# Early tiles of a routed two-layer network: row loads, pads, releases, and one expert's weight split on another engine

## The reference

```python
z = _layernorm(x, ln_g, ln_b)
logits = jnp.einsum('bth,he->bte', z, rW) + rb          # 8 experts
topv, topi = jax.lax.top_k(softmax(logits), 2)
w = mask / denom                                        # weights of the two chosen
hid = jax.nn.gelu(jnp.einsum('bth,ehf->btef', z, W1) + b1, approximate=False)
outs = jnp.einsum('btef,efh->bteh', hid, W2) + b2
mixed = jnp.sum(outs * w[..., None], axis=2)
return x + mixed
```

## Time and profile before

| | us |
|---|---|
| median of 3 runs | 565.91 (563.12 to 567.77) |
| the profiled execution | 563.68 |
| its span, first to last instruction | 561.6 |
| TensorE busy | 449.8 (80%) |
| DVE busy | 442.2 (79%) |
| ACT busy | 377.1 (67%) |
| POOL busy | 268.0 (48%) |
| mean granted TensorE clock | 0.930 |

### The profile page before, as it was taken

The page is one execution under the profiler, slowest core; times in us unless marked ns, Lnnn a source line. Parts: engine busy times, 40 slices in busy tenths (PEclk is TensorE's granted clock), DMA queues, the critical chain, the costliest instruction groups (busy, mean ns, idle before and its releaser), DMA issues.

```text
span 561.6 us, 11667 instructions
## 1 busy us (share of the span) xinstructions
PE 449.8 (80%) x2730; PEld 387.5 (69%) x2730; DVE 442.2 (79%) x1492; ACT 377.1 (67%) x928; POOL 268.0 (48%) x195
## 2 busy tenths in 40 slices
PE   0296899967999978588668999999999999999100
PEld 0146888846988867257557898999999999998100
DVE  6999795999898988874858777887888878887282
ACT  6992864446666657866535777777777777776184
POOL 0000359444566877564274344445444445444365
PEclk9997999999999997688978999999999999999655
DMA  6302730042224366496245457545544444444596
GB/s 168 134 1 100 298 127 1 0 131 77 104 95 171 141 218 207 121 350 207 49 128 96 76 97 176 80 75 85 84 79 78 77 77 77 77 77 53 146 403 269
DMA packets 47615, 70.35 MB, mean 125 GB/s; under 512 B 7616, under 2 KB 37184, under 8 KB 47040
## 3 DMA queue, kind: packets, MB, share of 16 engines
q1 hardware_dynamic: 34256, 51.82, 27.7%
q0 software_dynamic: 13296, 17.80, 19.0%
HBM read 37.90 MB, written 31.70 MB: 124 GB/s over the span
## 4 chain that ended last, share of the span: by engine, by line
PE 47%; DVE 25%; ACT 11%; issue 6%; DMA 5%; POOL 2%; SPq 2%; another core or an unknown queue 1%; DVEq 1%; POOLq 0%; ACTq 0%
PE psum L1487 15%; PE psum L1511 14%; PE psum L1497 5%; PE psum L1407 3%; DVE ws L934 3%; DMA yr<-y_rows 2%; PE psum L1471 2%; DVE st L739 2%; PE psum L1365 2%; ACT dump L652 2%; PE psum L1354 2%; PE psum L1355 1%; DVE o L1147 1%; ACT ws L589 1%; PE psum L1378 1%
## 5 line engine op out<-in xcount | busy, mean ns | idle before, releaser
L1316 POOL DMA_INDIRECT y_rows<-yw,dst x71 | 113.0, 1591 | 141.3 <-SPq L398 86.6
L1487 PE MATMUL psum<-ws,z_hl 128*128 x426 | 121.6, 422 | 6.2 <-issue 3.2
L1511 PE MATMUL psum<-ws,h_hl 128*128 x852 | 116.4, 286 | 0.6 <-DVE h_hl L1100 0.6
L1511 PEld LDWEIGHTS psum<-ws,h_hl 128*128 128x128 f32 x852 | 104.0, 189 | 0.8 <-issue 0.8
L1487 PEld LDWEIGHTS psum<-ws,z_hl 128*128 128x128 f32 x426 | 77.7, 196 | 22.2 <-issue 8.9
L1272 POOL DMA_INDIRECT z_rows<-zn,pos x64 | 71.0, 1110 | 27.4 <-issue 17.1
L597 ACT ACTIVATE z_f<-psum,gb 128x128 f32<-128x128 f32 x142 | 57.2, 453 | 17.5 <-issue 7.5
L634 ACT ACTIVATE hg<-hb 128x512 f32<-128x512 f32 x71 | 44.9, 633 | 31.1 <-DVE hb L1094 30.1
L1407 PE MATMUL psum<-yf,it 128*128 128x256 f32 x256 | 59.2, 387 | 2.6 <-DVE r L1121 2.6
L1081 DVE CAST z_hl<-z_f 128x256 fp32r<-128x256 f32 x71 | 21.0, 296 | 48.7 <-PE psum L1487 31.9
L1378 PE MATMUL psum<-pm,ft 128*128 128x256 f32 x256 | 58.2, 382 | 0.4 <-DVE tmp L920 0.2
(11 more groups left out here) (222 smaller groups left out, 841.2 us busy)
## 6 DMA issues: line engine op xcount, KB each, us to landing
z_in<-z_rows SPq DMA_DIRECT2D x71, 129.5 KB
w_raw<-in_dram SPq DMA_DIRECT2D x16, 512.0 KB, 5.9
xs<-in_dram SPq DMA_DIRECT2D x8, 512.0 KB, 5.4
x_dram<-xs SPq DMA_DIRECT2D x8, 512.0 KB
y_rows<-zn SPq DMA_DIRECT2D x8, 512.0 KB, 3.5
yr<-y_rows SPq DMA_DIRECT2D x8, 512.0 KB, 7.3
out_dram<-acc SPq DMA_DIRECT2D x7, 512.0 KB, 5.0
b1r<-in_dram SPq DMA_DIRECT2D x8, 256.0 KB
```

What stands on the lines that cost most here:

```text
L1316: pool.indirect_dma_start(y_rows, bass.IndirectOffsetOnAxis(ap=dst[t % 8][:, 0:1], axis=0), yw[t % 6][:, :], None, compute_op=ALU.add).the ...
L1487: last = TE.matmul(ps_h[q], z_hl[q][:, a, k], w_at(e, c, k * F, F), start=n == 0, stop=n == 5)
L1511: last = TE.matmul(ps_y[q], h_hl[q][:, a, k], w_at(e, c, 1024 + k * H, H), start=n == 0, stop=n == 11)
```

## The change

- DVE's subtraction for expert 6 goes to POOL, ahead of the 16 scatters of its step 8 (own semaphore `w_low_6`); ACT's cast for it goes from the middle of step 8 to its head. Tile 0's first layer waits for `w_low_6`.
- SP: in rows 6 and 7, the wait for `x1_stored` inside `store_rows` goes, and `load_z(2)` and `load_z(3)` stand between the stores. Tiles 4 to 13 are loaded in one loop; the eight pads stand two each after the loads of tiles 9 to 12, before one each after tiles 6 to 13. `release` is only used from tile 14 on.
- POOL: tiles 1 to 13 wait until the scatter of the tile before has landed, whatever the experts. `turns` for the early tiles goes.
- The copy of the destinations into `dst` goes (L1110); the scatter reads `row_of`.
- TensorE's step 8: `transposes(1)` ahead of two spins and `rank`, and six more spins ahead of `first_layer(0)`.
- ACT: one Gelu of a 128x1 operand ahead of row 7's `renormalise`; `enlarge` of row 7 ahead of `gelu(0)`.

```diff
@@ sync
-            store_rows(6, 7)
-            sp.wait_ge(sem("x1_ready"), B)
-            sp.dma_start(x1_dram[:, B - 1], xs[B - 1][:, :, :]).then_inc(sem("x1_stored"), 16)
-            load_z(2)
-            sp.wait_ge(sem("zn_ready"), B)
-            sp.dma_start(y_tok[:, B - 1], zn[buf(B - 1)][:, :, 0:H]).then_inc(sem(f"zn_stored{buf(B - 1)}"), 16)
-            load_z(3)
+            for b in (6, 7):
+                sp.wait_ge(sem("x1_ready"), b + 1)
+                sp.dma_start(x1_dram[:, b], xs[b][:, :, :]).then_inc(sem("x1_stored"), 16)
+                if b == 7:
+                    load_z(3)
+                sp.wait_ge(sem("zn_ready"), b + 1)
+                sp.dma_start(y_tok[:, b], zn[buf(b)][:, :, 0:H]).then_inc(sem(f"zn_stored{buf(b)}"), 16)
+                if b == 6:
+                    load_z(2)
...
-            load_z(4)
-            load_z(5)
-            for t in range(6, FIRST):
+            for t in range(4, FIRST):
                 load_z(t)
-                if t > 6:
-                    release(t - 6)
-                if t == 6:
+                if t == 9:
                     sp.wait_ge(sem("pad_set"), 1)
-                pad(t - 6)
+                if 9 <= t < 13:
+                    pad(2 * (t - 9))
+                    pad(2 * (t - 9) + 1)
...
             for t in range(FIRST, TILES):
                 load_z(t)
-                release(t - 6)
+                if t - 6 >= FIRST:
+                    release(t - 6)
@@ scalar, step
                 inv, cur, tail = (Row(n, k) for k in (0, -1, -2))
+                if n == B:
+                    split_high(6)
...
                 if tail.live:
                     renormalise(tail)
-                if n == B:
-                    split_high(6)
...
                     scaled(1)
+
+                    nc.scalar.activation(wt[5][:, :], eps[:, 0:1], ACT.Gelu)
                     renormalise(cur)
...
             settle(0)
+            enlarge(Row(B, -1))
             gelu(0)
-            enlarge(Row(B, -1))
@@ vector
-                turns(1, FIRST, tf_h)
...
-                V.tensor_copy(dst[t % 8][:, :], row_of[:, t:t + 1])
...
                     row(0)
-                    split_low(6)
                     choose(tail)
@@ gpsimd, step
                 elif n == B:
+
+                    pool.wait_ge(sem("w_high"), 7)
+                    G.tensor_tensor(ws[:, 6, 1], w_raw[6][:, :], ws[:, 6, 0].bitcast(F32), ALU.subtract).then_inc(sem("w_low_6"), 1)
                     scatter(last_tail, 0, 8)
                     scatter(tail, 0, 8)
@@ gpsimd, scatter_y
-                if t:
-                    pool.wait_ge(sem("released"), t)
+                if t >= FIRST:
+                    pool.wait_ge(sem("released"), t - FIRST + 1)
+                    gate(pool)
+                elif t:
+                    pool.wait_ge(sem(f"y_out{1 - q}"), ((t - 1) // 2 + 1) * 16)
                     gate(pool)
...
-                pool.indirect_dma_start(y_rows, bass.IndirectOffsetOnAxis(ap=dst[t % 8][:, 0:1], axis=0),
+                pool.indirect_dma_start(y_rows, bass.IndirectOffsetOnAxis(ap=row_of[:, t:t + 1], axis=0),
@@ tensor, first_layer
                 if t in (0, FIRST):
-                    pe.wait_ge(sem("w_low"), E - 1 + (t == FIRST))
+                    pe.wait_ge(sem("w_low"), E - 2 + (t == FIRST))
+                if t == 0:
+                    pe.wait_ge(sem("w_low_6"), 1)
@@ tensor, step
                 if n == B:
+                    transposes(1)
                     spin(2, 0)
                     rank(tail)
-                    transposes(1)
+                    spin(6, 0)
                     first_layer(0)
```

More of the change, by code:

```diff
@@ L154, in program @@
     tab_e = at("tab_e", [P, TILES + 1], F32, c0 + 5952)
-    dst = [at(f"dst{i}", [P, 1], U32, o0 + 71 * KB + 256 + 32 * i) for i in range(8)]
     row_of = at("row_of", [P, TILES + 1], U32, o0 + 71 * KB + 736)
```

## The result

| | kernel before | changed kernel |
|---|---|---|
| median, us (runs) | 565.73 (4) | 581.62 (4, 578.62 to 584.64) |
| ratio, 95% interval | | 1.0284 (1.0208 to 1.0360) |
| profiled execution, time / span | 563.68 / 561.6 | 584.64 / 582.8 |

Slower by 15.9 us in the medians; 563.0 (558.0 to 569.5) was forecast.

The account below looks back on a forecast made before the run. DVE was taken to bound the early tiles, TensorE the late ones. Head +4.6, `share` -4.7, `tell` -1.1, tile 14's load -1.1, copies -0.6: net -2.9, 560.8 beside 563.68, 563.0 beside the median; range 558.0 to 569.5.

Parts of the forecast that it names:

- What bounds the kernel: TensorE sets late tiles at 3.41 us each; before about tile 11 DVE sets the pace, with 6.9 us of waits.
- Head, +4.6: Before tile 0: POOL's subtraction holds DVE and six spins delay TensorE, so the head ends 4.6 us later.
- rival (e): Head: spins run at the low clock after TensorE idles, +5 us, 568; chance 0.07.
- Rival (b): Step 8: POOL's subtraction doesn't hold DVE, head only +0.5, total 558.9; chance 0.12.
- `share`, `tell`, tile 14 and copies, -7.5: Early tiles: waits in two long tiles and at tile 14's load vanish, copies go: -4.7, -1.1, -1.1, -0.6 us.
- the 4.7: Tile of `share`: 4.7 us beyond DVE's own work, part SP's stop at the pads, part late releases; all won back.
- The 1.1 at tile 14's load: Row load 14 no longer stands behind the wait for all pads, saving 1.1 us in DVE's distance.
- The landing chain, 0: POOL's scatter-adds of tiles 2 to 13, each awaiting the last landing, end at 345.7; buffer slack covers it, no cost.
- (c): POOL's chain of scatters becomes the bound at pitch 5 or more, giving 3 to 5 us back, 567; chance 0.07.
- (a): Early tiles: late releases stay with the eight scatters, 5.8 us of gains fall away, 568.8; chance 0.26.
- (d): Whole kernel: DVE isn't held but late releases stay, everything hidden or given back, -1.2, 564.7; chance 0.08.
- ACT waiting for `y_out`: Sign named for a wrong forecast: ScalarE waiting in `weigh` for a scatter's landing; no size given.

Follow-up runs that it names:

- p_before: Kernel before, unchanged, profiled again beside the others of its call on another chip; ratio 1, the reference there.
- group B: Sets of runs on two further chips, where the kernel before took 559.8 to 559.9 us.
- group A: The result and one set each on two chips, where the kernel before took 565.7 to 566.1 us.
- a_late_release: Changed kernel with SyncE's release of a late tile put behind the row load eight tiles on instead of six; ratio 1.0177.
- p_after: Changed kernel, unchanged, profiled beside the kernel before on the same chip; ratio 1.0349.
- b_spin: Kernel before with tile 1's transposes moved ahead and six spins between row 6's rank and tile 0's first layer; ratio 1.0052.
- a_released: Changed kernel with tiles 1 to 13 again released one by one by SyncE instead of waiting on GpSimd for the landing before; 570.89 us, ratio 1.0095.
- b_serial: Kernel before with only the landing waits of tiles 1 to 13 on GpSimd, SyncE releasing from tile 14 on; ratio 1.0271.
- c_mix_block: As c_mix, but with the last batch row's eight row scatters in one block ahead of tile 2; ratio 0.9936.
- c_mix: Changed kernel without spins, seventh expert as before, landing waits only for tiles 1 to 5, row scatters two each ahead of tiles 2 to 5; 557.12 us, ratio 0.9867.
- b_rows: Kernel before with only the change's row-load order and pads, and no copy into dst; ratio 0.9934.
- b_rows_spread: As b_rows, with the last batch row's eight row scatters two each ahead of tiles 2 to 5; ratio 0.9880.
- a_chain_spread: Changed kernel with the last batch row's eight row scatters two each ahead of the scatter-adds of tiles 2 to 5; ratio 1.0224.

## Why the prediction was wrong, point by point

1. **What bounds the kernel**: right for the late tiles (3.44 us each, nothing given back or won from tile 19 on). For the early tiles the long tile of `share` was read as a property of the kernel. It belonged to that execution: in p_before the length stands at tile 8, and that the sum of tiles 3 to 10 is the same (41.3 and 41.0 us) is luck, as the two causes differ.
2. **Head, +4.6**: measured +5.0 in the pair of group B (263.13 to 268.17), +4.6 to +10.3 in group A's executions of the same head (a_late_release 270.13, changed kernel 275.84, against 265.50). The steps held: L1130 4.15 ("about 4"), spins 5.40 us at a granted clock of 1.00 in p_after ("5.3"). In the first profile four things came on top: the step began 1.05 late, the logits' result was late (1.80 at 250.80), the spins ran at 0.76 (7.09), and the turn's result was late again (ended 262.43, used 264.31), after which TensorE was at half clock. So rival (e) happened in that execution and not in the other, with 1.7 us (7.09 against 5.40) rather than 5 for the spins. The Trainium skill (TensorE: Matmul & The Clock Gate, Part 1) ties the low clock to idleness ahead; the executions agree with it: 1.62 us of idleness ahead of the rank and the spins at 0.76 (7.09), 1.93 in b_spin (7.09 and 0.76 too), none in p_after (1.00, 5.40). Not every such gap did it: 1.15 us in a_released left the spins at 5.40.
   The Trainium skill's shared port pair (SBUF — State Buffer, Who interferes with whom), held for the whole instruction, is what the rows show: 4.49 us of subtraction, both ends within 0.02 us. Rival (b) is out.
3. **`share`, `tell`, tile 14 and copies, -7.5**: from tile 2 to tile 17 the changed kernel took 59.42 and the kernel before 65.14 in group B, -5.7; in the first profiles 62.42 and 66.57, -4.2; in a_released 65.26, -1.3. The sign was right, the size and the place were not. SyncE's stop at the pads was worth 0.1 in the tile of `share`; it cost time through tile 1's release and the block, at tile 8 (8.62, p_after 3.23). The late results of TensorE, the rest of the 4.7, stayed in group A. The 1.1 at tile 14's load came exactly in the first profiles (tile 11: 3.43 for 4.55), but in group B there was nothing to win (3.44 for 3.46). A copy is worth the 0.06 of the forecast where VectorE sets the pace (tile 8: 3.22 for 3.28), but the 0.6 in sum doesn't show: tiles 8 to 10 took 9.91 for 9.84.
4. **The landing chain, 0**: this is the step that failed. The prediction put the last landing at 345.7 and the time when it is wanted at 344.9, "its buffer is wanted again by tile 19". Landing: 353.3, about 6.2 later because tile 2 went out at 295.2 and not 289, and 2.6 because of a pitch of 4.94 instead of 4.7; minus 1 for a shorter landing. Wanted: 339.0, by SyncE, not by the buffer. The change leaves `release` of tile 14 between row loads 20 and 21, and `order` makes it wait for tile 13. The prediction had noted that SyncE "has then fewer waits" and did not ask what the first remaining one waits for. In the clock of the kernel before that is 333, 12 us ahead of the time assumed. It cost 13.4 us (first profile), 16.6 (b_serial) and 19.8 (p_after). The chain is most of the miss; the rest of the sum was off too. Without the chain the changed kernel was still 0.95% slower (a_released, 0.54 to 1.36), where 0.5% faster was forecast.
5. **The rivals**: (c) names the mechanism, at 0.07 and with 3 to 5 us. It alone is 2.7% (b_serial). (a), late releases staying, came true in group A (11.21 for the tile of `share` in a_released, and 3.4 us between c_mix_block and c_mix) and not in group B (6.09 in p_after). Its 568.8, 0.5% slower, is somewhat under what a_released measured (0.95%), and far from the changed kernel's time. (d) is out.
6. **What was to show it**: "ACT waiting for `y_out`" was named as the mark of the failed chain. ScalarE never waited for it; TensorE and VectorE waited for a row load. The mark was looked for in the wrong queue. Another mark was there: L1316's starts were to be 4.2 to 4.7 apart, and were 4.94 on average.

Left open: why TensorE's results arrive up to 6 us after their record during the block of eight, on the chips of group A and not on those of group B. Taking the block apart ends it in tiles 3 to 5; what the two share was not tried. The head shows the same mark. In every trace of group A ScalarE or VectorE waits over 1 us with releaser "remote" beside the sixteen row scatters of step 8 or within 2 us of their end (ScalarE until 262.73 in the kernel before and 262.15 in c_mix, for example), and in no trace of group B. This is part of why tile 0 varies between executions. Of the 5.7 us between the changed kernel's first profile and a_late_release, which have one head, 1.8 lie ahead of row 6's mask (252.46, 250.67), 1.7 in the spins and 2.2 behind them. It isn't all: b_rows and b_rows_spread, both of group B, differ by 6.0 at tile 0, and 4.1 of it stand already at step 8's L1130 (227.98, 232.10). Why the pipeline ahead of step 8 varies so was not looked into.

## What to carry to other kernels

When waits are moved from one queue to another, list for each wait that remains which event it now asks for, and work out its time against the moment the queue comes there, not against the last user of the data. A chain of landings at 4.9 us a link under a stage of 3.4 us a tile loses 1.5 us each tile; here it was hidden up to the first in-order queue that waited for its end, and the row loads behind that wait stopped as well. Before pricing a gain from one long tile of one profile, look at it in a second execution.

## What the hardware showed

- A scatter-add of 128 rows issued alone took 1.6 us on GpSimd and in most cases landed 3.7 to 3.9 us after its start (single ones 4.5 and 5.4, in the changed kernel and a_late_release); the next that waited for it began 4.7 to 4.9 after it. With two row scatters of 1.3 us put into that gap the steps were 5.1, 5.0 and 5.5 (285.96, 291.05, 296.06, 301.52 in a_chain_spread): they were nearly free there, and 10.3 us as a block.
- TensorE's results reached ScalarE and VectorE late, up to 6 us after the end of their records, while eight indirect scatters ran in a row. This cost 3.4 us in tiles 3 to 5 in group A (c_mix_block 19.6, c_mix 16.2) and nothing in group B (b_rows 16.1 with the block).
- A long wait of TensorE cost more than its length: 11.89 us at tile 21's row load made tile 18 13.4 us longer, with a granted clock of 0.68 for the 5.6 us behind it.
- The kernel before took 565.7 to 566.1 us in three sets and 559.8 to 559.9 in two others; a difference of 1% between kernels can only be read within one set.
